# 24 instead of 16 of 33 expert pairs with split down projections, with PSUM banks and small steps moved between engines

## The reference

```python
h = _L0_tok_ref(x, ...)                                   # 8 x 512 tokens, 128 channels
h = h + _L0_attn_ref(_layernorm(h), ...)                  # decayed linear attention, then a small gelu block
h = h + _L0_ffn_ref(_layernorm(h), ...)                   # 1 shared pair of experts and 64 routed ones, top 6
...
router_probs = jax.nn.softmax(router_logits, axis=-1)
topk_p, topk_i = jax.lax.top_k(router_probs, K)
...
hg = jnp.einsum('ecd,efd->ecf', expert_in, w_gate)
hu = jnp.einsum('ecd,efd->ecf', expert_in, w_up)
expert_out = jnp.einsum('ecf,edf->ecd', jax.nn.silu(hg) * hu, w_down)
```

## Time and profile before

| what | value |
|---|---|
| time, median of 3 runs | 718.22 us (716.77 lowest, 1065.27 highest) |
| span of the profiled execution, first to last instruction | 716.0 us |
| PE busy | 692.8 us, 97% of the span, 3133 matmuls |
| DVE, POOL, ACT busy | 73%, 65%, 49% of the span |

### The profile page before, as it was taken

One profiled execution on the slowest core, in us unless ns is written; L12 is line 12 of the kernel. 1 busy time (PEld: TensorE's weight loads), 2 busy tenths in 40 slices (PEclk: granted clock), 3 DMA queues, 4 the chain that ended last, 5 costly groups with the idle time before them and its releaser, 6 DMA issues.

```text
span 716.0 us, 9975 instructions
## 1 busy us (share of the span) xinstructions
PE 692.8 (97%) x3133; PEld 524.7 (73%) x3133; DVE 523.4 (73%) x1074; ACT 350.6 (49%) x609; POOL 466.5 (65%) x345
## 2 busy tenths in 40 slices
PE   7788899999999999999999999999999999999998
PEld 7666677777777777777777777777777777777775
DVE  5677686987768867887769877788678766674444
ACT  3543455446454374445553474544745435534432
POOL 5035477776677767685676776676775656676664
PEclk9999999999999999999999999999999999999999
DMA  5504232243323333333333433333333433334431
GB/s 204 226 1 128 71 118 104 85 133 105 111 106 114 114 108 99 120 113 102 118 103 101 128 103 103 118 110 109 114 105 102 125 103 105 115 112 124 138 123 60
DMA packets 48869, 80.17 MB, mean 112 GB/s; under 512 B 9520, under 2 KB 13744, under 8 KB 48816
## 3 DMA queue, kind: packets, MB, share of 16 engines
q1 hardware_dynamic: 47792, 77.44, 33.4%
q0 software_dynamic: 1024, 2.10, 1.2%
HBM read 76.35 MB, written 3.15 MB: 111 GB/s over the span
## 4 chain that ended last, share of the span: by engine, by line
PE 88%; DVE 4%; issue 3%; POOL 2%; ACT 1%; DVEq 0%; POOLq 0%
PE bank_y L467 16%; PE bank_g L481 8%; PE bank_g L482 8%; PE bank_g L483 8%; PE bank_u L483 8%; PE bank_u L481 8%; PE bank_u L482 8%; PE bank_y L464 4%; PE bank_y L462 4%; PE bank_y L461 4%; POOL hid L1040 1%; PE bank_f L408 1%; PE bank_f L386 1%; PE bank_f L402 1%; PE bank_f L445 1%
## 5 line engine op out<-in xcount | busy, mean ns | idle before, releaser
L1040 POOL TENSOR_TENSOR hid<-hid,gate_rows 128x512 f32<-128x512 f32 x256 | 374.2, 1470 | 195.4 <-DVE hid L881 193.0
L623 ACT ACTIVATE hid<-bank_g 128x512 f32<-128x512 f32 x264 | 156.6, 599 | 264.4 <-PE bank_g L483 261.8
L881 DVE TENSOR_TENSOR hid<-hid,bank_u 128x512 f32<-128x512 f32 x264 | 178.7, 681 | 128.3 <-PE bank_u L483 78.2
L481 PE MATMUL bank_g<-x_hi,gate_hi 128*128 128x512 f32 x264 | 142.9, 541 | 0.0
L467 PE MATMUL bank_y<-hid,w_down 128*128 128x512 f32 x272 | 138.7, 591 | 0.0
L887 DVE TENSOR_TENSOR hid_lo<-hid,hid_hi 128x512 fp32r<-128x512 f32 x128 | 110.2, 861 | 2.4 <-ACT hid_hi L629 2.4
L482 PE MATMUL bank_g<-x_hi,gate_lo 128*128 128x512 f32 x264 | 104.5, 396 | 0.0
L483 PE MATMUL bank_g<-x_lo,gate_hi 128*128 128x512 f32 x264 | 104.5, 396 | 0.0
L481 PE MATMUL bank_u<-x_hi,up_hi 128*128 128x512 f32 x264 | 103.9, 393 | 0.1
L483 PE MATMUL bank_u<-x_lo,up_hi 128*128 128x512 f32 x264 | 103.8, 393 | 0.0
L482 PE MATMUL bank_u<-x_hi,up_lo 128*128 128x512 f32 x264 | 103.8, 393 | 0.0
(11 more groups left out here) (209 smaller groups left out, 857.1 us busy)
## 6 DMA issues: line engine op xcount, KB each, us to landing
gate_rows<-gates_dram SPq DMA_DIRECT2D x512, 128.0 KB, 2.9
w_down<-down_t_dram SPq DMA_DIRECT2D x3, 704.0 KB, 14.5
out_dram<-later SPq DMA_DIRECT2D x7, 256.0 KB, 3.1
hid<-gate_t_dram SPq DMA_DIRECT2D x2, 704.0 KB, 5.8
gates_dram<-gates_t SPq DMA_DIRECT2D x8, 128.0 KB, 2.2
gate_rows<-up_t_dram SPq DMA_DIRECT2D x1, 704.0 KB, 5.7
later<-up_t_dram SPq DMA_DIRECT2D x1, 704.0 KB, 9.9
raw<-gate_t_dram SPq DMA_DIRECT2D x1, 704.0 KB, 11.0
```

The lines of the kernel that those rows point to most:

```text
L481: pe.matmul(o, w_hi[name][:, p, :], x3_hi[par][:, :], start=True, stop=False)
L623: act.activation(hid[:, slot(par, p), :], bank_g[(p + par) % 2][:, :], ACT.Silu).then_inc(sem("silu"), 1)
L881: dve.tensor_tensor(hid[:, s, :], hid[:, s, :], bank_u[(p + par) % 2][:, :], ALU.mult)\
L1040: pool.tensor_tensor(hid[:, s, :], hid[:, s, :], gate_rows[:, row, :], ALU.mult)\
```

## The change

The split set becomes every pair whose number is not a multiple of four: 24 pairs instead of 16 (new are 2, 6, 10, ..., 30). The rings hid_hi and hid_lo get three slots. bank_y becomes one bank, with a wait for its copy (ffn_t) ahead of each batch's first down, and the copy moves up a position; bank_u becomes three. x1 goes from DVE to ACT, and so does xn2 from batch 1 on. The additions var3 and var1 go from DVE to POOL, and POOL computes two more small steps (shift1) for x1's new form. In the start-up stretch three pairs are put ahead of the first gates_t, not two.

```diff
-SPLIT_LAG, SPLIT_RING = 2, 2
-SPLITS = PAIRS // 2
+SPLIT_LAG, SPLIT_RING = 2, 3
+SPLIT_PAIRS = tuple(p for p in range(PAIRS) if p % 4)
+SPLITS = len(SPLIT_PAIRS)
...
-DVE_AT = dict(xn=0, xn_lo=2, x1=5, xn_dec=5, y_lo=4, scores=6, state=6, x2=8, result=10, logits=9, xn2=11, exp_sum=12,
+DVE_AT = dict(xn=0, xn_lo=2, xn_dec=5, y_lo=4, scores=6, state=6, x2=8, result=10, logits=9, xn2=11, exp_sum=12,
...
-ACT_AT = dict(xn_hi=2, y_hi=4, z=6, ffn_t=5, squares=9, squares2=10, cluster_exp=10, exp_t=12, xn2_t=13, vals=14,
+ACT_AT = dict(xn_hi=2, y_hi=4, x1=5, z=6, ffn_t=4, squares=9, squares2=10, cluster_exp=10, xn2=11, exp_t=12, xn2_t=13, vals=14,
...
-AHEAD = 3
+AHEAD = 4
...
-        bank_u = [bank(f"bank_u{i}") for i in range(2)]
-        bank_y = [bank(f"bank_y{i}") for i in range(2)]
+        bank_u = [bank(f"bank_u{i}") for i in range(3)]
+        bank_y = bank("bank_y")
...
-            y = bank_y[par][:, :]
+            y = bank_y[:, :]
+            if p == 0:
+                wait(pe, "ffn_t", b)
...
-                wait(pe, freed, q - 1)
-                o = banks[ring][:, :]
+            for name, out_bank, freed, count in (("gate", bank_g[q % 2], "silu", q - 1),
+                                                 ("up", bank_u[q % 3], "up_used", q - 2)):
+
+                wait(pe, freed, count)
+                o = out_bank[:, :]
...
+            if p == ACT_AT["x1"]:
+
+                act.wait_ge(sem("shift1"), b + 1)
+                wait(act, "x2", b)
+                for t in range(TILES):
+                    last = act.activation(x1[:, t, :], emb[par][:, t, :], ACT.Identity,
+                                          bias=shift1[:, t:t + 1], scale=inv1[:, 0, t:t + 1])
+                last.then_inc(sem("x1"), 1)
+            if p == ACT_AT["xn2"] and b:
+                act.wait_ge(sem("inv2"), b + 1)
+                for t in range(TILES):
+                    last = act.activation(xn2[:, t, :], x2[:, t, :], ACT.Copy, scale=inv2[:, t:t + 1])
+                last.then_inc(sem("xn2"), 1)
...
-            wait(act, "down_done", q - 2 * SPLIT_RING + 1)
-            act.activation(hid_hi[:, (p // 2) % SPLIT_RING, :], hid[:, slot(par, p), :], ACT.Copy)\
+            wait(act, "down_done", split_slot_freed(b, p))
+            act.activation(hid_hi[:, split_slot(b, p), :], hid[:, slot(par, p), :], ACT.Copy)\
...
-                    act.activation(down_hi[:, :, :], odd_pairs(w_down), ACT.Copy).then_inc(sem("down_hi"), 1)
+                    act.activation(by_fours(down_hi), split_pairs(w_down), ACT.Copy).then_inc(sem("down_hi"), 1)
...
             if p == POOL_AT["inv3"]:
+                pool.wait_ge(sem("mv3"), b + 1)
+                pool.tensor_scalar(var3[:, :], mv3[:, :, 1], LN_EPS, None, ALU.add).then_inc(sem("var3"), 1)
                 pool.wait_ge(sem("var3"), b + 1)
...
             if p == POOL_AT["inv1"]:
+                pool.wait_ge(sem("mv1"), b + 1)
+                pool.tensor_scalar(var1[:, 0, :], mv1[:, :, 1], LN_EPS, None, ALU.add)
+                pool.tensor_scalar(var1[:, 1, :], mv1[:, :, 1], 1.0 + RMS_EPS, RMS_EPS * LN_EPS, ALU.mult, ALU.add)\
+                    .then_inc(sem("var1"), 1)
+                wait(pool, "x1", b)
                 pool.wait_ge(sem("var1"), b + 1)
...
+                pool.wait_ge(sem("inv1"), b + 1)
+                pool.tensor_tensor(shift1[:, :], mv1[:, :, 0], inv1[:, 0, :], ALU.mult).then_inc(sem("shifts"), 1)
+                pool.wait_ge(sem("shifts"), b + 1)
+                pool.tensor_scalar(shift1[:, :], shift1[:, :], -1.0, None, ALU.mult).then_inc(sem("shift1"), 1)
```

More of the change, by code:

```diff
@@ L162, in build @@
         inv1 = sb("inv1", [P, 2, TILES])
+        shift1 = sb("shift1", [P, TILES])
         x1 = sb("x1", [P, TILES, D])
+        decay_full = x1[:, 0, :]
         xn = sb("xn", [P, TILES, D])
         xn2_t = sb("xn2_t", [P, SEQ])
-        vals = sb("vals", [P, SEQ])
+        vals = xn2_t
         turns = sb("turns", [P, 2 * (TILES - 1) * P])
@@ L281, in split_lo @@
                 dve.wait_ge(sem("down_hi"), 1)
-                dve.tensor_tensor(down_lo[:, :, :], odd_pairs(w_down), down_hi[:, :, :].bitcast(F32), ALU.subtract)\
+                dve.tensor_tensor(by_fours(down_lo), split_pairs(w_down), by_fours(down_hi[:, :, :].bitcast(F32)), ALU.subtract)\
                    .then_inc(sem("down_lo"), 1)
@@ L475, in gate_up @@
                     pe.wait_ge(sem(f"split_lo{CHUNK_OF[n, p]}"), 1)
-            ring = (p + par) % 2
-            for name, banks, freed in (("gate", bank_g, "silu"), ("up", bank_u, "up_used")):
-                wait(pe, freed, q - 1)
-                o = banks[ring][:, :]
+            if b == 0 and p == 2:
+                pe.wait_ge(sem("h"), 2)
+            for name, out_bank, freed, count in (("gate", bank_g[q % 2], "silu", q - 1),
+                                                 ("up", bank_u[q % 3], "up_used", q - 2)):
+                wait(pe, freed, count)
+                o = out_bank[:, :]
                 pe.matmul(o, w_hi[name][:, p, :], x3_hi[par][:, :], start=True, stop=False)
@@ L541, in _ @@
             for p in range(PAIRS):
-                pe_early(pe, 0, p, bank_y)
+                pe_early(pe, 0, p, first_banks)
                 if p == PE_AT["exp_t"]:
@@ L562, in _ @@
                     gate_up(pe, 0, 0, AHEAD - 1)
-                pe_early(pe, 1, p - SHIFT, bank_y)
-                warm(pe, bank_y[1] if p >= PE_AT["gates_t"] else bank_u[1], WARM.get(p, 0))
+                pe_early(pe, 1, p - SHIFT, first_banks)
+                warm(pe, bank_y if p >= PE_AT["gates_t"] else bank_u[1], WARM.get(p, 0))
             sequences(pe, lambda *a: pe_sequence(pe, *a))
@@ L633, in act_copy_out @@
             act.wait_ge(sem("down_done"), PAIRS * b + PAIRS)
-            act.activation(ffn_t, bank_y[par][:, :], ACT.Copy).then_inc(sem("ffn_t"), 1)
+            act.activation(ffn_t, bank_y[:, :], ACT.Copy).then_inc(sem("ffn_t"), 1)
         def act_sequence(act, b, par, late, early):
@@ L667, in _ @@
             for p in range(PAIRS):
-                act_early(act, 0, p, bank_y)
+                act_early(act, 0, p, first_banks)
                 split_hi(act, p - PAIRS)
@@ L687, in _ @@
                 c = slice(k * SEQ // 2, (k + 1) * SEQ // 2)
-                act.activation(ffn_t[:, c], bank_y[1][:, c], ACT.Copy).then_inc(sem("ffn_half"), 1)
+                act.activation(ffn_t[:, c], bank_y[:, c], ACT.Copy).then_inc(sem("ffn_half"), 1)
         def dve_late(dve, b, par, p):
@@ L699, in dve_late @@
                 last.then_inc(sem("xn"), 1)
-            if p == DVE_AT["x1"]:
-                for t in range(TILES):
-                    last = dve.tensor_scalar(x1[:, t, :], emb[par][:, t, :], mv1[:, t, 0:1], inv1[:, 0, t:t + 1],
-                                             ALU.subtract, ALU.mult)
-                last.then_inc(sem("x1"), 1)
             if p == DVE_AT["xn_dec"]:
@@ L742, in dve_late @@
                    .then_inc(sem("x2"), 1)
-            if p == DVE_AT["xn2"]:
+            if p == DVE_AT["xn2"] and b == 0:
                 dve.wait_ge(sem("inv2"), b + 1)
@@ L762, in dve_late @@
                 last.then_inc(sem("mv3"), 1)
-                dve.wait_ge(sem("mv3"), b + 1)
-                dve.tensor_scalar(var3[:, :], mv3[:, :, 1], LN_EPS, None, ALU.add).then_inc(sem("var3"), 1)
             if p == DVE_AT["x3"]:
@@ L905, in dve_sequence @@
                     split_lo(dve, PAIRS + p)
+                if first and p == 0:
+                    dve_up(dve, b, par, AHEAD - 2)
                 if p >= AHEAD - 1 or not first:
```

43 lines of the change are left out of this document (24 added, 19 removed).

## The result

The changed kernel takes 746.89 us (median of 4 runs, 746.72 to 748.05); before it was 717.87 us beside them. The ratio is 1.0414, 95% interval 1.0399 to 1.043: slower by 4%. The profiled execution has a span of 746.2 us, 30.2 more than before. The forecast was 717.5 with a range of 705 to 728, so the time lies far outside.

What follows compares the result with a forecast made beforehand. PE was taken as the bound, busy 82.5 of a batch's 83.0 us. The terms -10.6 - 2.5 + 11.7 + 1.1 gave -0.3 us: span 715.7, median 717.9, written as 717.5; range 705 to 728.

Steps and rivals of the forecast that it cites:

- The splits: PE's down matmuls: 8 more split pairs in 8 batches, 0.165 us less each, 10.6 us less.
- Rival C: PE waits for hid_lo at the third matmul of new split pairs, so splits gain nothing: 723.9 us; chance 0.11.
- x1 on ACT: PE's wait ahead of state at position 6, 0.49 us in five batches, goes as DVE is earlier: 2.5 us less.
- The way to the gates: From inv1 on POOL to gates_t on PE: DVE and POOL come later, PE waits 1.8 us per batch, 11.7 more.
- both waits: PE's waits at the gate_up of pair 26 and at gates_t, together 1.8 us per batch in six batches.
- the upper end: Upper end, 2.8 us, for the low parts of pairs 22 and 26 between logits and gates; 0.6 was taken.
- Start: Start-up stretch: first gates 2.5 us later, of which batch 0 regains 1.4 ahead of state; 1.1 us more.
- Rival B: The wait gathers at gates_t and PE's clock falls behind it, each batch: 740.7 us; chance 0.09.
- Its point of decision: The clock-fall case at gates_t decides from about 2.2 us of waiting in one piece; there the time is 728.7.

Runs made afterwards that it cites:

- best3: best2 with inv1 on POOL two positions later (22, not 20), behind the multiplies of pairs 20 and 21: 711.9 us, ratio 0.9917.
- lo3: Changed kernel with the low part of pair 3 behind the next batch's scores on DVE, not ahead of them: 729.49 us, ratio 1.0151.
- x1dve: Changed kernel with the four operations of x1 back on DVE at position 5, small operations still on POOL: 750.3 us, ratio 1.0445.
- dvevar: Changed kernel with the small operations around inv1 and inv3 back on DVE, x1 and xn2 still on ACT: 736.04 us, ratio 1.0254.
- plain3: Changed kernel with pairs 2, 22 and 26 as one full-precision matmul each again (21 split pairs): 733.37 us, ratio 1.0225.
- ahead3: Changed kernel with two pairs ahead of the first gates again, not three: 745.22 us, ratio 1.0376.
- odd16: Changed kernel with only the 16 odd pairs split, as before the change; down weights still split for 24: 729.06 us, ratio 1.0167.
- splits24: Changed kernel with x1, xn2 and small operations on DVE and two pairs ahead, as before the change; 24 splits and banks stay: 740.31 us, ratio 1.0313.
- best2: Changed kernel with pair 3's low part behind scores, small operations on DVE, two pairs ahead, prob, top, chosen, gates earlier, down weights' low half in three parts: 716.15 us.

## Why the prediction was wrong, step by step

**The splits, -10.6.** Right in kind and nearly in size: -8.4 in the changed kernel, -9.7 by the batch of best3 (8 x (81.30 - 0.16 - 82.35)). Some 1 us of that difference are the matmuls right behind the waits, which the first row of the table counts. Rival C, a price at the third matmul of the split pairs, did not come: 0.6 us in all.

**x1 on ACT, -2.5: the step that failed.** The wait ahead of state was to vanish; it grew by 7.8 us and drew 6.2 us of fallen clock behind it, 16.5 of the 30.5 us between the forecast span and the measured one. "x1 leaves DVE, one dve_lo (pair 2) comes in, 0.68 to 1.41 us: DVE is earlier by at least 1.8, so the wait goes". Two assumptions are in it. The first: that 3.22 us of x1 were DVE's work to be had back. On an idle POOL the same four take 1.11 us (the first row below, from the start-up stretch of the kernel before), so two thirds were standing behind POOL, and that passes to the operation on SBUF operands that comes next. The second: that a low part costs at most 1.41. The same trace has low parts of 2.17 us a little ahead of x1 (the second row below, pair 1, and so in five batches), which the forecast did not take; behind two multiplies in a row it is 3.1 to 3.5.

```profile
24.46 1.11 DVE L703 TENSOR_SCALAR x<-emb,mv,inv 128x128 f32<-128x128 f32 x4
...
398.83 2.17 DVE L887 TENSOR_TENSOR hid_lo<-hid,hid_hi 128x512 fp32r<-128x512 f32 x1
```

lo3 shows it by moving that one operation (17.4 us expected; 17.4 between the medians, 17.9 with each taken against its own runs of the kernel before), x1dve by bringing x1 back: state comes 0.35 us later, not 2.9. POOL's own order of time beside the earlier trace rows would have told it: 4 gathers and 4 multiplies from 395.54 to 405.71 with no pause over 0.2 us, then 1.1 us of idling that x1 itself had caused.

**The way to the gates, +11.7.** The place was right, both waits were named, and the size was off: 19.7. The logits come 2.0 us later against the router's matmuls, not 0.95: POOL's small operations cost 1.71 us instead of the assumed 1.0 (one of them took 0.67, not 0.19), and the low part behind took 1.10. dvevar shows the share at gate_up 26 (1.53 to 0.2), plain3 that at gates_t (the low parts of pairs 22 and 26, 1.2 us instead of the 0.6 taken, but well under the 2.8 of the upper end). At the seventh hand-over, which has no inv1 block, the wait at gates_t was 0.94 us, and 0.9 had been forecast.

**Start, +1.1.** The first gates_t was to come 2.5 us later and came 5.25 later (60.52 against 55.27). The forecast counted the longer high half of the down weights on ACT, 0.95, but not the low half behind it on DVE, which takes 2.0 us more; on DVE the gates were ready 2.4 us later (57.62). PE was to be through with gate_up and the transposes before that, and was not: the silu of pair 0 came 2.4 us later too, behind the wait for it the granted clock was 0.57, and gate_up and transposes took 5.25 us instead of 3.75. ahead3 gives 2.8 us back. Of the 1.4 us that batch 0 was to regain ahead of state it regained 0.34.

**Rival B, slower because the clock falls**, had the sign and the mechanism but the wrong place. Its point of decision, 2.2 us in one piece, was looked for at gates_t, where no wait was over 1.3; the long wait, 2.07 us, was at state, which the forecast had struck out. There the Trainium skill's rule that stood beside rival B (SBUF — State Buffer, Who interferes with whom) was to be applied too: a VectorE instruction with two SBUF inputs and a GpSimd one that reads SBUF shut each other out. The rows here agree (3.12 us beside two multiplies, 0.68 beside none, 0.76 for the scores with an operand in PSUM). That the one that starts later waits, as the prediction cites it, can't be read from the starts in the trace: the low part of odd16 started 0.41 us ahead of the multiplies and took 3.51 us.

**What stays open.** What decides whether the clock falls behind the wait at state: after 2.07 us it fell in 4 of 5 batches of the changed kernel and of ahead3 and, after 2.07 to 2.11, in none of dvevar, where the wait of 1.53 us some 37 us earlier was missing; after 2.4 us in 5 of 5 batches of x1dve and 2 of 5 of splits24. No run varied it alone. The start's last 2 us were not recovered by best2, so what sets them is not shown. That gathers fill POOL's stretch is shown only by the batch that has none; no run moved them.
